# Gated linear attention with a mixture of experts on one core: the state update turned, and an expert's gate and up matrices loaded on their own

## What is computed

```python
xn = _layernorm(x)
# attention: keys of 128, values of 64, one decay per token and head
state = at[..., None, None] * state + kt[..., None] * vt[:, :, None, :]
out_t = jnp.einsum('bhk,bhkv->bhv', qt, state)
att = (out * og) @ Wo                      # og = sigmoid(xn @ Wog)
# experts: 8 of 64 for each token, at most 256 tokens for each expert
g = jnp.einsum('ech,ehi->eci', buf, w_gate)
u = jnp.einsum('ech,ehi->eci', buf, w_up)
y = jnp.einsum('eci,eih->ech', silu(g) * u, w_down)
x = x + att + ffn
```

## Time and profile before

| | |
|---|---|
| median of 3 runs | 1294.01 us (1293.33 to 1294.12) |
| the profiled execution | 1293.95 us; its span from first to last instruction 1292.1 us |
| PE busy | 1269.3 us (98%) |
| PE weight loads | 1125.7 us (87%) |
| DVE busy | 938.7 us (73%) |
| ACT busy | 555.5 us (43%) |
| POOL busy | 474.0 us (37%) |
| granted TensorE clock, mean | 0.996 of full speed |

### The profile page before, as it was taken

How to read it: one execution, slowest core, us unless ns; L and a number is a source line. 1 busy time by engine, 2 the same in 40 slices (tenths; PEclk the granted TensorE clock), 3 DMA queues, 4 the chain that set the end, 5 groups by cost and what they waited for, 6 DMA issues and landing times.

```text
span 1292.1 us, 27351 instructions
## 1 busy us (share of the span) xinstructions
PE 1269.3 (98%) x9542; PEld 1125.7 (87%) x9542; DVE 938.7 (73%) x2215; ACT 555.5 (43%) x1131; POOL 474.0 (37%) x377
## 2 busy tenths in 40 slices
PE   7999999999999999999999999999999999999999
PEld 6788888888888888899888999898899899989887
DVE  6987979889796559778577666775775766756834
ACT  6565646565663433333333333333333333333322
POOL 2110101011011027246366374573662744645710
PEclk8999999999999999999999999999999999999999
DMA  6566534363352312367486475774764747747755
GB/s 243 174 240 202 173 103 167 122 200 124 128 163 74 112 50 83 110 152 171 101 202 139 122 182 118 175 177 101 184 159 119 185 105 179 167 113 157 182 171 195
DMA packets 124917, 194.64 MB, mean 151 GB/s; under 512 B 12016, under 2 KB 98608, under 8 KB 124592
## 3 DMA queue, kind: packets, MB, share of 16 engines
q1 hardware_dynamic: 94384, 147.99, 35.4%
q0 software_dynamic: 30464, 45.83, 19.3%
HBM read 148.62 MB, written 57.74 MB: 160 GB/s over the span
## 4 chain that ended last, share of the span: by engine, by line
PE 83%; DVE 11%; issue 3%; DMA 1%; ACT 1%; DVEq 0%; SPq 0%; ACTq 0%
PE bank L752 23%; PE bank L835 7%; PE bank L802 7%; PE bank L885 7%; PE bank L853 7%; PE bank L767 7%; PE bank L784 5%; PE bank L820 5%; PE bank L894 4%; PE bank L823 4%; PE bank L793 3%; PE bank L875 2%; DVE Dt L1412 2%; DVE At L1433 1%; PE bank L682 1%
## 5 line engine op out<-in xcount | busy, mean ns | idle before, releaser
L594 POOL DMA_INDIRECT acc<-arena,idx_all x128 | 216.6, 1692 | 131.2 <-issue 54.6
L586 POOL DMA_INDIRECT arena<-table,idx_all x132 | 157.4, 1192 | 204.7 <-ACT share L1094 147.1
L752 PE MATMUL bank<-xp,wq 128*128 128x512 f32 x768 | 214.7, 415 | 0.0
L752 PE MATMUL bank<-xp,wk 128*128 128x512 f32 x768 | 202.3, 398 | 0.2 <-DVE wk L1322 0.2
L752 PEld LDWEIGHTS bank<-xp,wk 128*128 128x128 f32 x768 | 141.9, 188 | 34.2 <-DVE wk L1322 0.6
L752 PEld LDWEIGHTS bank<-xp,wq 128*128 128x128 f32 x768 | 141.0, 190 | 27.8 <-issue 0.5
L1412 DVE TENSOR_TENSOR_SCAN Dt<-decay,eye_b 128x512 f32<-128x512 f32 x128 | 157.2, 1230 | 0.0
L802 PE MATMUL bank<-qT,kT 128*128 128x128 f32 x1024 | 135.5, 275 | 1.8 <-DVE At L1433 1.8
L1074 ACT ACTIVATE qT<-bank 128x512 f32<-128x512 f32 x128 | 76.8, 600 | 129.2 <-PE bank L752 125.1
L802 PEld LDWEIGHTS bank<-qT,kT 128*128 128x128 f32 x1024 | 125.0, 192 | 2.7 <-DVE At L1433 2.1
L835 PEld LDWEIGHTS bank<-V,kw 128*128 128x128 f32 x960 | 117.5, 191 | 11.2 <-issue 10.1
(11 more groups left out here) (167 smaller groups left out, 2194.5 us busy)
## 6 DMA issues: line engine op xcount, KB each, us to landing
decay<-decay_dram SPq DMA_DIRECT2D x64, 512.0 KB
carry<-decay_dram SPq DMA_DIRECT2D x60, 512.0 KB
arena<-in_L_attn_x_dram SPq DMA_DIRECT2D x16, 512.0 KB, 4.5
table<-arena SPq DMA_DIRECT2D x16, 512.0 KB, 3.7
xT_dram<-arena SPq DMA_DIRECT2D x16, 512.0 KB, 3.0
arena<-in_L_ffn_w_gate_dram SPq DMA_DIRECT2D x64, 128.0 KB
arena<-in_L_ffn_w_up_dram SPq DMA_DIRECT2D x64, 128.0 KB
arena<-in_L_ffn_w_down_dram SPq DMA_DIRECT2D x64, 128.0 KB
```

The costliest lines, as they stand in the source:

```text
L586: pool.indirect_dma_start(out=xg[:, e % 2, j, :], out_offset=None, in_=table[:, :], in_offset=bass.IndirectOffsetOnAxis(ap=idx_all[:, e, j ...
L594: pool.indirect_dma_start(out=acc[:, :], out_offset=bass.IndirectOffsetOnAxis(ap=idx_all[:, e, j:j + 1], axis=0), in_=yb[:, e % 2, j, :], ...
L752: last = mm(to[:, :], w[:, part, k, h * DK:(h + 1) * DK], xp[:, other, k, :], start=(k + i == 0), stop=(k == KD - 1 and i == 2))
```

## The change

Four things change in the kernel.

1. **The update is turned** in the steps "count", "slots" and "experts" (ten steps, four pairs each). After the even substep's projections, ahead of the outputs, `update_turned` makes the products of both heads of the pair: the 64 values are stationary, on one column half for each head, and the 128 key columns move; result in bank 3. ACT copies bank 3 into the second half of `kw` (`update_copy`), and after the outputs PE turns it back into bank 6 with four transposes (`update_back`). `kw` gets two halves. `keys_back` of an even head also waits for this copy. DVE's add reads bank 6 in another order. The "norm" steps keep the old update.
2. **Loads.** Gate and up have a semaphore of their own and are loaded when the split of the expert two before is done (`wgu_split`), down still after `y_ps`. PE waits for the down matrix itself. SP's order in "experts" steps is written anew.
3. **ACT's order.** In "experts" steps the high part of the weights (L1101) comes behind the update's copy.
4. **In "count"** the output gate projection stands behind the keys' projection.

```diff
+            def update_turned(c, p):
+                pe.wait_ge(kw_cp, at(c, 8, 2 * p + 2))
+                pe.wait_ge(v_cp, 4 * c + 4)
+                for b in range(B):
+                    for u in range(2):
+                        h = 2 * p + u
+                        last = mm(bank[3][u * DV:(u + 1) * DV, b * P:(b + 1) * P], V[:, b, h * DV:(h + 1) * DV],
+                                  kw[:, u, b, :], start=True, stop=True)
+                last.then_inc(ut_ps, 1)
+            def update_back(c, p):
+                pe.wait_ge(ut_cp, 4 * (c - S_COUNT) + p + 1)
+                if p > 0:
+                    pe.wait_ge(state_up, at(c, 4, p))
+                else:
+                    pe.wait_ge(wo_cp, 4 * c)
+                for b in range(B):
+                    last = tr(bank[6][:, b * P:(b + 1) * P], added_t[:, b, :], ident[:, :])
+                last.then_inc(u_ps, 1)
...
             def keys_back(c, kind, h):
+                if turned(kind) and h % 2 == 0:
+                    wait_past(pe, ut_cp, 4 * (c - S_COUNT) + h // 2)
...
                     beside(c, kind, s, 2)
+                    if s % 2 == 0 and turned(kind):
+                        update_turned(c, s // 2 - 1)
                     if s % 2 == 0:
                         outputs(c, s // 2 - 1)
                     beside(c, kind, s, 4)
-                    if not is_last(c):
+                    if s % 2 == 0 and turned(kind):
+                        update_back(c, s // 2 - 1)
+                    if kind == "norm":
                         update(c, s - 1)
...
+            def update_copy(c, p):
+                act.wait_ge(ut_ps, 4 * (c - S_COUNT) + p + 1)
+                f(added_t.rearrange("p b d -> p (b d)"), bank[3][:, :], ACT.Copy).then_inc(ut_cp, 1)
...
             def pair_state(c, kind, p):
+                if turned(kind):
+                    summed = state[:, 2 * p:2 * p + 2]
+                    added = bank[6][:, :].rearrange("p (b u v) -> p u b v", b=B, u=2)
...
-            def next_expert(c, j):
+            def next_gate_up(c, j):
+                e = (c - E0) * STEP_E + j
+                sp.wait_ge(wgu_split, e + 1)
+                load_gate_up(e + 2, j % 2)
+            def next_down(c, j):
                 e = (c - E0) * STEP_E + j
                 sp.wait_ge(y_ps, e + 1)
-                load_expert(e + 2, j % 2)
+                load_down(e + 2, j % 2)
...
+            def step_experts(c):
+                load_decay(c, 3)
+                next_gate_up(c, 0)
+                next_gate_up(c, 1)
+                next_down(c, 0)
+                load_carry(c, 1)
+                load_xs(c + 1)
+                next_gate_up(c, 2)
+                load_decay(c + 1, 0)
+                next_down(c, 1)
+                next_gate_up(c, 3)
+                next_down(c, 2)
+                load_carry(c, 2)
+                next_gate_up(c, 4)
+                load_decay(c + 1, 1)
+                next_down(c, 3)
+                next_gate_up(c, 5)
+                next_down(c, 4)
+                load_carry(c, 3)
...
```

More of the change, by code:

```diff
@@ L316, in tokens_bank, with turned @@
             return bank[6] if is_first(c) and k == 1 else bank[7]
+        def turned(kind):
+            return kind in ("count", "slots", "experts")
         def og_slots(kind):
@@ L457, in step @@
                     norm_io(STEP_N * c + 3, more)
[L458 to L460 removed]
+            def step_experts(c):
+                ends = STEP_E if not isinstance(c, int) else STEP_E - 2
+                load_decay(c, 3)
[16 more added lines that the diff above has]
+                load_carry(c, 3)
+                if ends > 6:
+                    next_gate_up(c, 6)
+                load_decay(c + 1, 2)
+                next_down(c, 5)
+                if ends > 6:
+                    next_gate_up(c, 7)
+                    next_down(c, 6)
+                load_carry(c + 1, 0)
+                if ends > 6:
+                    next_down(c, 7)
             for name, (_, src) in split_of.items():
@@ L477, in _ @@
             sp.wait_ge(idx_ready, 1)
-            load_expert(0, 0)
-            load_expert(1, 1)
+            for e in range(2):
+                load_gate_up(e, e)
+                load_down(e, e)
             with sp.Fori(E0, E1 - 1) as c:
-                step(c, "experts")
-            step(E1 - 1, "experts")
+                step_experts(c)
+            step_experts(E1 - 1)
             load_decay(C - 1, 3)
@@ L1131, in beside @@
                     expert_gate(c, s - 1)
-                    if s < H:
-                        weights_high_e(c, s)
+                if kind == "experts" and 0 < s < H and place == 3:
+                    weights_high_e(c, s)
             def step(c, kind):
@@ L1172, in step @@
                         qk_copy(c, kind, s, 1)
+                    if s % 2 == 0 and kind in ("count", "slots"):
+                        update_copy(c, s // 2 - 1)
                     if kind == "norm" and s % 3 == 0:
@@ L1177, in step @@
                     beside(c, kind, s, 2)
+                    if s % 2 == 0 and kind == "experts":
+                        update_copy(c, s // 2 - 1)
+                    beside(c, kind, s, 3)
                     if s % 2 == 0:
@@ L1470, in pair_state @@
                 dve.wait_ge(u_ps, at(c, 4, p) + 1)
-                tt(both, both, added, ALU.add).then_inc(state_up, 1)
+                tt(summed, summed, added, ALU.add).then_inc(state_up, 1)
             def outs_low(c, p):
```

50 lines of the change are left out of this document (24 added, 26 removed).

## The result

| | before | after |
|---|---|---|
| median, on one chip, in turns | 1293.76 us (1293.33 to 1294.12) | 1277.56 us (1276.66 to 1277.98) |
| span of the profiled execution | 1292.1 us | 1275.8 us |
| PE busy | 1269.3 us | 1253.5 us |

A forecast was written before the change was run, and what follows sets the result against it. PE bounds nine of the ten changed steps, DVE the slots step. Experts 11.4 + count 1.6 + slots 0 + loads 1.6 = 14.6 us, from 1293.95 to 1279.3 us; range 1276.5 to 1285.5, about 0.85.

The forecast's parts named there:

- The turned products: On PE at the outputs: 16 instructions a pair at 0.055 us, 0.88 us, against 1.78 for the update removed.
- The transposes back: On PE behind the outputs: four 128x128 transposes, 0.44 us plus 0.11 taken over from the old update, 0.55 us a pair.
- The switch: PE's change into the column halves and out: paid once a pair before and after, so no term.
- Count: The count step: 1.4 us saved, plus 0.22 us of standstill in its last substep now filled, 1.6 us.
- Slots: The slots step: DVE sets the pace with its work unchanged, so 0 us, from -0.5 to +0.3.
- The late load of step 13: End of step 13, L885 started 1.54 us late; the earlier issue removes this, 1.6 us (between 0 and 1.6).
- The other 21 waits: ACT's weight copy waited for loads 22 times, 17.2 us in all; all but one were absorbed and give nothing.
- Rival 1: New small PE waits in odd substeps, 0.1 to 0.3 us over the spare time: 1282.5 to 1289 us; chance 0.12.
- everything upstream repeats to 0.01 us: Argument against new small waits in odd substeps: upstream work repeats to 0.01 us in the rows and nothing is made longer.
- Rival 2: Late carries: DVE stands at L1438, then PE; one load a step, 1 us beyond, costs 8 us: 1287 us; chance 0.04.
- Rival 3: Halves don't overlap: a turned instruction costs 0.11 us, a pair 1.76, 35 us in all, 1314 us; chance 0.04.
- Rival 4: Less gain: another load late instead, or the switch paid twice (0.15 us x 40 = 6 us): 1281 to 1285; chance 0.08.

The follow-up runs named there:

- `grouped`: The changed kernel with the four turned products of the lower column half first, then the four of the upper: 1296.22 us, ratio 1.0004 to the kernel before.
- `apart`: The changed kernel with the experts steps' turned products moved ahead of the gate and up projections: 1292.8 us, ratio 0.998 to the kernel before.
- `loads_only`: The kernel before with only the changed kernel's loads, semaphores and SP order, update not turned: 1292.37 us, ratio 0.9975.
- `order_only`: `turned_only` with nothing but the carries moved behind the weights in SP's order: 1280.85 us, ratio 0.9886 to the kernel before.
- `one_earlier`: The changed kernel with the loads' new conditions, but SP's old order, carries ahead of the loads: 1300.58 us, ratio 1.0034 to the kernel before.
- `turned_only`: The changed kernel with the loads and SP's order of before, all three matrices loaded behind `y_ps`: 1301.9 us, ratio 1.0043 to the kernel before.
- `turned_act_old`: `turned_only` with ACT copying the weights ahead of the update again, as in the kernel before: 1296.35 us, ratio 1.0003 to the kernel before.

## Why the prediction was right, and where its argument was not

**Direction and size** came out: 16.2 us against 14.6, at 1277.56 us. Step by step it was 17.1, and the 2.5 us that the sum lacks are 1.9 in the experts steps (14.9 against 13.0), 0.75 in count and 0.16 in the norm steps, less 0.25 in slots. By one of its own signs the prediction was wrong: an experts step was to be shorter by 1.3 to 1.5 us and is shorter by 1.62.

**The turned products** at 0.055 us an instruction: 0.92 us a pair against 0.88; the outputs behind them take 0.04 less (1.85 instead of 1.89), so the two together came out as summed. `grouped` shows that the reason given, alternation of halves as in L820, is the right one.

**The transposes back** were mis-sized: 0.50 and not 0.55. Entering the whole array behind the halves was taken from the old update (0.11); behind transposes it costs 0.06. 0.05 us in each of 32 pairs is 1.6 of the 1.9 us that the experts steps gained beyond the sum.

**The switch** as no term: right, since the place at the outputs saves one; `apart` shows 0.35 us a pair as the price of one more.

**Count** gained 2.35 and not 1.6. The step that failed took L835's 0.83 us in all odd substeps; in three of count's four it stood behind column-half products and took 0.94 (423.70 to 424.64), and the odd substeps lost 0.85 to 0.96 us each.

**Slots** lost 0.25 and stayed within its -0.5 to +0.3: odd substeps 0.32 to 0.34 us shorter, waiting for the keys' copy (the four waits shown), even ones 0.46 to 0.48 longer.

**The late load of step 13** went: 1.78 us, forecast 1.6. But "The other 21 waits were absorbed by idle time of ACT and DVE and give nothing" is the sentence that failed. It is true of the profiled execution of the kernel before, as `loads_only` shows, though the medians (3.1 us) leave room for more in others. And it was carried over to shorter substeps without being tested against them: the spare time ahead of gate and up falls from 2.14 to 1.54 us in the even substeps and from 0.73 to 0.15 in the eighth, and loads that are up to 3.6 us late then cost 24 us. The forecast came out because the change brings both parts at once. It also credited the wrong detail: the earlier condition was said to do it, while 21 of the 24 us come from the carries' place in SP's queue (`order_only`, `one_earlier`), which the prediction weighed only as a risk.

**Rival 1** didn't happen in the odd substeps, where it was looked for: PE has no wait row at L952 or L942. It happened in small in the eighth, 0.12 us a step, 1 us in all; "everything upstream repeats to 0.01 us" doesn't hold there, where the spare time before went from 0.15 to 0.73. **Rival 2** didn't: there is no idle time of DVE ahead of `ends_kept`, and SP issues the carry right behind the weights. **Rival 3** is right about one half and wrong about two. **Rival 4** is `apart` for its second half: it would have been 14 us, not 6, some 11 for the trips (32 x 0.35) and the rest mostly for the wait at the end of the step.

**Left open.** Why `turned_only` swings between 1294 and 1306 us from run to run, and whether the spare time or SP's longer stand at the carry (156 us in 24 waits against 115 before) does more of its harm. Both follow from the turning, and no run parts them.

## What to carry to other kernels

A wait that an engine absorbs is absorbed only at the present length of its surroundings: before shortening the path beside it, compare the wait with the spare time that will be left, and test each half of such a change alone. In a queue that issues in order, a cheap load with its condition met can stand behind one whose condition comes late; put it ahead. Half-array products should alternate between the halves and stand next to others of their kind, or, in this kernel, they cost as much as what they replace.

## What the runs showed of the hardware

- Half-array fp32 instructions (64 stationary, 128 moving columns): 0.055 us each when the halves alternate, 0.11 us when one half has several in a row; products of the other half fit into the gaps.
- One more trip from whole-array products into the halves and back costs 0.35 us (`apart`, 6.53 against 6.18 us); ahead of four transposes the way out costs 0.06 us (0.50 against 0.44).
- 128 KB loads issued behind 1 MB of other loads were there only 7.7 us after their issue (`turned_only`, 780.51 to 788.24).
- Kernels with late loads spread from run to run: `turned_only` by 11.9 us, `one_earlier` by 13.7 (1294.69 to 1308.36), `turned_act_old` by 11.0, the kernel before by 7.1 on one chip (1291.86 to 1298.98). Those with loads in time keep within 1 to 3 us (`order_only` 1280.4 to 1283.36).
